# Graph layers on one core: attribute loads, table clears and window addresses moved ahead of the barrier behind the sorting

## The reference

```python
# layer 0, attention (edge_index = [src, dst], adj_vals = edge_weight)
h = x @ W
score = h[src] @ a_src + h[dst] @ a_dst
edge_e = exp(-leaky_relu(score, 0.2)) * adj_vals
h_prime = segment_sum(edge_e[:, None] * h[dst], src) / segment_sum(edge_e, src)
return elu(h_prime)
...
# layer 1, three rounds
for i in range(3):
    msg = relu(x[src] + edge_attr)
    aggr = segment_sum(msg, dst)
    h = relu(bn((x + aggr) @ W1[i] + b1[i]))
    x = bn(h @ W2[i] + b2[i])          # relu too, but for i = 2
```

## Time and profile before

| | us |
|---|---|
| median of 3 runs (lowest, highest) | 4825.21 (4821.34, 4827.64) |
| profiled execution, its own time | 4826.38 |
| its span | 4824.7 |
| PE busy, DVE busy, ACT busy, POOL busy | 4257.5, 4048.8, 2655.3, 3255.8 |
| sorting ends (ACT's last low, L841) | 793.7 |
| block 0 of the attention, first score | 810.1 |
| left-over step of the attention, DVE | 939.2 |
| end of the attention on PE | 2014.7 |

### The profile page before, as it was taken

How to read it: one execution, slowest core, us unless ns; L and a number is a source line. 1 busy time by engine, 2 the same in 40 slices (tenths; PEclk the granted TensorE clock), 3 DMA queues, 4 the chain that set the end, 5 groups by cost and what they waited for, 6 DMA issues and landing times.

```text
span 4824.7 us, 143705 instructions
## 1 busy us (share of the span) xinstructions
PE 4257.5 (88%) x50439; PEld 4143.0 (86%) x50440; DVE 4048.8 (84%) x7870; ACT 2655.3 (55%) x6749; POOL 3255.8 (67%) x2584
## 2 busy tenths in 40 slices
PE   2576676699999999789999997999999979999998
PEld 2566675699999999779999996999999969999996
DVE  7899996477777777678888887888888888888887
ACT  3899996377777777633344345334333454434434
POOL 0488883577777777557777773677777537777763
PEclk7777777799999999889999999999999989999999
DMA  9957663999899888678888884888888848888884
GB/s 123 263 187 242 205 217 124 306 251 251 248 249 250 252 249 248 176 239 278 281 280 279 280 280 149 265 280 281 278 277 281 265 151 279 281 279 280 280 281 148
DMA packets 664741, 1183.55 MB, mean 245 GB/s; under 512 B 151850, under 2 KB 489596, under 8 KB 664588
## 3 DMA queue, kind: packets, MB, share of 16 engines
q1 hardware_dynamic: 450204, 839.07, 53.1%
q10 hardware_dynamic: 133200, 176.14, 15.0%
q0 software_dynamic: 81184, 166.43, 11.0%
HBM read 967.32 MB, written 214.44 MB: 245 GB/s over the span
## 4 chain that ended last, share of the span: by engine, by line
PE 69%; DVE 16%; issue 6%; SPq 5%; DVEq 2%; ACT 1%; DMA 1%; POOL 0%; ACTq 0%; POOLq 0%; PEld 0%; PEldq 0%
PE ps L1766 23%; PE ps L1752 16%; PE ps L1681 12%; PE ps L1668 10%; PE ps L1776 6%; DVE sums L1159 2%; DVE field L1159 2%; DVE dst_hot L1452 2%; DVE sums L1460 2%; DVEq L1465 1%; SPq L552 1%; PE ps L1818 1%; DVE blk_hot L1151 1%; DVE scan L1196 1%; DVE rank L1213 1%
## 5 line engine op out<-in xcount | busy, mean ns | idle before, releaser
L774 POOL DMA_INDIRECT unit_x<-gin_rows,unit_src x1449 | 1785.1, 1232 | 701.8 <-PE ps L1766 456.8
L729 POOL DMA_INDIRECT attr_by_slot<-abuf,ridx x1080 | 1411.7, 1307 | 534.9 <-issue 327.4
L1766 PE MATMUL ps<-dst_hot,sums 128*128 128x128 f32 x10584 | 1519.8, 284 | 84.7 <-DVE agg L1467 84.7
L969 ACT ACTIVATE sums<-sums 128x512 f32<-128x512 f32 x1512 | 834.0, 572 | 1283.0 <-DVE sums L1460 1279.2
L1766 PEld LDWEIGHTS ps<-dst_hot,sums 128*128 128x128 f32 x10584 | 1306.4, 192 | 103.0 <-DVE agg L1467 86.1
L1752 PE MATMUL ps<-x_parts,src_turned 128*128 128x128 bf16 x15876 | 1143.0, 220 | 37.4 <-POOL x_parts L761 33.2
L1752 PEld LDWEIGHTS ps<-x_parts,src_turned 128*128 128x128 bf16 x15876 | 1026.8, 99 | 56.9 <-issue 41.6
L1460 DVE TENSOR_TENSOR sums<-ps,sums 128x512 f32<-128x512 f32 x1512 | 903.7, 615 | 131.2 <-PE ps L1752 127.5
L1452 DVE TENSOR_TENSOR dst_hot<-iota_one,dl_slot 128x896 f32<-128x896 f32 x756 | 818.2, 1082 | 2.2 <-DVE agg L1505 2.2
L881 ACT ACTIVATE val<-ps,val 128x128 f32<-128x128 f32 x2597 | 717.9, 375 | 185.2 <-DVE val L1305 185.2
L1681 PE MATMUL ps<-val,src_hot 128*128 128x129 f32 x5194 | 694.7, 283 | 2.2 <-DVE sums L1245 1.0
(11 more groups left out here) (243 smaller groups left out, 4361.3 us busy)
## 6 DMA issues: line engine op xcount, KB each, us to landing
sums<-attr_by_slot SPq DMA_DIRECT2D x756, 448.0 KB
src_turned<-rows_by_group SPq DMA_DIRECT2D x756, 224.0 KB
turned_hot<-rows_by_block ACTq DMA_DIRECT2D x392, 384.0 KB
attr_by_slot<-zeros SPq DMA_DIRECT2D x36, 3136.0 KB
unit_attr<-in_edge_attr SPq DMA_DIRECT2D x204, 448.0 KB
abuf<-in_edge_attr SPq DMA_DIRECT2D x72, 960.0 KB
unit_x<-gin_rows,unit_src POOLq DMA_INDIRECT x1449
attr_by_slot<-abuf,ridx POOLq DMA_INDIRECT x1080
```

Source lines behind the costliest of these rows:

```text
L729: pool.indirect_dma_start(out=attr_table, out_offset=bass.IndirectOffsetOnAxis(ap=ridx[:, g, t0 + t:t0 + t + 1], axis=0), in_=abuf[:, k % ...
L774: pool.indirect_dma_start(out=unit_x[:, half_place(k), t, :], out_offset=None, in_=gin_rows[n], in_offset=bass.IndirectOffsetOnAxis(ap=uni ...
L969: act.activation(attr[:, first:first + tiles, :], attr[:, first:first + tiles, :], ACT.Relu).then_inc(s_msg, 1)
L1766: ins = pe.matmul(ps[:, 7, 0:WINDOW], attr[:, b, :], dst_hot[:, HOT[c], b % G_TILES, :], start=(b == 0), stop=(b == BLOCKS - 1))
```

## The change

SORT_LOADS goes from 16 to 18, so loads 16 and 17 stand ahead of the barrier. LOADS_THEN goes from 19 to 20, so one more half is loaded and scattered ahead of the left-over step. The 34 clears are spread over the first 14 loads (CLEAR_LOADS) in place of 19. The first rows of the first 12 windows (HELD) behind the barrier are read into registers ahead of the waits.

```diff
-LOADS_THEN = 19
-SORT_LOADS = 16
+LOADS_THEN = 20
+SORT_LOADS = 18
+CLEAR_LOADS = 14
+HELD = 12
...
-            def load_windows(c):
+            def window_base(g):
+                return sp.value_load(base_i[0:1, g:g + 1], min_val=0, max_val=NODES - 1)
+
+            def load_windows(c, held={}):
                 for g in range(c * A_TILES, c * A_TILES + a_tiles(c)):
-                    base = sp.value_load(base_i[0:1, g:g + 1], min_val=0, max_val=NODES - 1)
+                    base = held[g] if g in held else window_base(g)
                     sp.dma_start(window_of(g), att_rows[bass.ds(window_at(base), WINDOW), :]).then_inc(s_win[c], 16)
...
                 if k == SORT_LOADS:
 
+                    held = {g: window_base(g) for g in range(EARLY * A_TILES, EARLY * A_TILES + HELD)}
                     sp.wait_ge(s_fld, GROUPS)
...
                     for c in range(EARLY, A_CHUNKS):
-                        load_windows(c)
+                        load_windows(c, held)
                 load_half(k)
-                for g in range(k * (BUCKETS - FILLS_FIRST) // LOADS_THEN, (k + 1) * (BUCKETS - FILLS_FIRST) // LOADS_THEN):
-                    clear_slots(g + FILLS_FIRST)
+                for g in range(k * (BUCKETS - FILLS_FIRST) // CLEAR_LOADS, (k + 1) * (BUCKETS - FILLS_FIRST) // CLEAR_LOADS):
+                    if g + FILLS_FIRST < BUCKETS:
+                        clear_slots(g + FILLS_FIRST)
```

## The result

| | before | changed |
|---|---|---|
| median of the runs (lowest, highest), us | 4825.72 (4821.34, 4827.64) | 4783.28 (4780.17, 4784.3) |
| ratio, 95% interval | | 0.9914 [0.9902, 0.9926] |
| profiled execution: its own time, span | 4826.38, 4824.7 | 4784.3, 4782.6 |

The change makes the kernel faster by 0.9%, 42 us; the forecast was 4778, 47 us. Lines behind the edit stand 7 further down (L1725 is now L1732, L1293 is L1300, L588 is L594).

The account below looks back on a forecast made before the run. PE was taken to stand 36.1 us before the left-over step for POOL's late gather, and block 0 to wait for windows; 36.1 + 8.0 + 3.0 = 47.1 us off 4825.2 gave 4778, own range 4773 to 4785.

Parts of the forecast that it names:

- Loads 16 and 17: SP's queue ahead of the barrier: issued at about 736 and 775 us, so POOL scatters on without waiting for data.
- The barrier: SP's wait ahead of the windows: still ends at 793 to 794 us; later than 795 would speak for starved scatters.
- Twelve reads ahead: SP's windows behind the barrier: end 8.5 us earlier, and block 0 of the attention gains 8.0, bounds 0 and 9.5.
- The rival of full engines: Block 0: DMA engines, not SP, set when windows land, so the reads bring nothing; gain 39.1 us, 4786, chance 9%.
- PE's wait: PE ahead of the left-over step: its whole wait of 36.1 us for POOL's gather goes.
- the clears: SP's queue in the sorting: denser clears hide under POOL's step with 5 us to spare, costed at nothing.
- The clock: PE behind the left-over step: without the hole, time at the lower clock goes too; 3.0 us, bounds 0 to 6.
- POOL's end: End of attention: POOL's scatters set it if POOL starts no earlier; gain 17 us, 4808, chance 3%.
- The late gather: Left-over step: four halves ahead of the gather make it late again; gain 40 to 47 us, up to 4785, chance 6%.
- the slower case: Sorting and barrier: denser clears starve POOL and delay load 17, barrier and windows; 4835 or more, chance 2%.
- no change: Whole kernel: the saved time comes back somewhere unseen, a change under 0.2%; chance 3%.

Follow-up runs that it names:

- g2: Changed kernel with POOL waiting until all slots are added before it scatters half 16, nothing left out: 4783.45 us, ratio 0.9914.
- g1: The kernel before, unchanged, run again for its profile: 4823.64 us (one run).
- g3: Kernel before with the clears over the first 14 loads and the 12 reads ahead, its loads unchanged: 4792.5 us, ratio 0.9934.
- g4: Changed kernel without POOL's scatters from half 20 on, 780 of 1080 left out: 4784.87 us, ratio 0.9918.
- e4: Kernel before with only the twelve reads ahead of the barrier, on the chip where the kernel before takes 5226 us: 5220.19 us, ratio 0.9987.
- e2: Kernel before with only the 34 clears spread over the first 14 loads, on the 5226 us chip: 5212.15 us, ratio 0.9967.

## Why the prediction was right, and where its sizes were off

The mechanism held, the sum was 6.4 us too large in the attention (47.1 against 40.7); the median, 4783.28, lies inside the forecast's own range of 4773 to 4785, 1.7 us from its upper end. The table splits the 40.7 into score 4.95, blocks 1 and 2 -0.24, idle 34.49 and rest 1.48.

**Loads 16 and 17** went early and met no barrier, as forecast; the last ended at 775.7 (775). POOL scattered from 774.4 to 816.5 without a hole (774 to 819).

**The barrier** opened at 795.1, against 793 to 794 forecast. That isn't starved scatters: the kernel before gives 794.56 in one execution and 795.49 in another, and holding the scatters back (g2) gives 794.23.

**Twelve reads ahead.** I took 8.5 us for SP and 8.0 for block 0. SP's windows went from 40.6 to 35.1 us: 5.5. Here one step failed, the guess that the old excess of the first 12 windows over their step was the reads' and would go as well: with the reads gone these 12 still take 804.5 - 795.1 = 9.4 us, and their DMA instruction itself takes 0.51 us at the median and up to 1.13 on SP, where that of the other windows takes 0.33. So even the 7.2 us of 12 x 0.6 didn't come whole. Block 0 gained 4.95 against the one profile of before and 6.41 against g1. From the first window's DMA to the last score it took 48.8 and 49.4 us before, and 42.6 to 43.7 in the four kernels with reads ahead, so 5 to 7 us is what the 12 reads give, at most 0.6 us each. The rival of full engines had foreseen no gain here; its share was 0.97 from 794 to 811 us and the windows landed in 3.2/4.0/6.6 us (min, median, max) where the earlier trace rows show 2.0/3.5/6.5, so the landing took back a part, not all. The rule of the Trainium skill that I weighed (DMA: Bandwidth & Descriptors, Issuing engines are not separate DMA queues) has that much in it here.

**PE's wait** was to go whole; 1.6 us stayed, in every kernel on the first chip that has the loads early. The trace puts it down to "issue". In the changed kernel DVE's first operation of the step is at 897.94 and its one-hot at 899.05, so DVE was ready for PE by then. The gather went at 881.6 (forecast 877), since data for half 18 were there at 839.35 in place of 835.4. It had 11 us to spare: in g3, where it is late, PE's product followed the second gather by 8.75 us, and 881.58 + 8.75 is 890.3.

**What removes the wait.** I gave the whole of it to the data that come earlier and costed the clears at nothing. That they cost nothing was right: SP issues a load and three clears in about 17 us in a step of 37.5, and POOL's idle time stays 0.30. That they bring nothing was wrong, and it was in my own rows: the full queues were read there. By g3 the clears and the reads alone take the gather to 899.0 and leave 11.4 us of the wait; only these are the loads'. In the medians that is 31.6 us and 9.1. (Between the two profiled executions it is 6.5: 9.75 less of the wait, and block 2 later by 3.57. Of that 1.98 is a later first window, and this start lies anywhere from 793.2 to 796.1 in the six executions, with early loads or without.) Clears and reads weren't run apart on this chip; by the table the reads' part is 5 to 7 us of the 31.6. Whether the loads alone would do as well as the clears alone wasn't tried there either.

**The clock** was to give 3.0 us, and gave nothing that can be told from the spread. Block 3 takes 918.07 - 903.35 = 14.7 us from chunk 0 to chunk 5 behind an idle time of 1.63, and 957.44 - 942.78 = 14.7 in g1, behind 32.77; the 15.9 of the profile that I used was 1.2 above what another execution of the same kernel shows, and g2, g3 and g4 show 15.0, 14.7 and 14.6. Timeline of DVE of g1:

```profile
942.78 0.18 DVE L1293 TENSOR_REDUCE z<-ps 128x6 f32<-128x24 f32 x1 [0.89 <-DVE sums L1375]
...
957.44 0.18 DVE L1293 TENSOR_REDUCE z<-ps 128x6 f32<-128x24 f32 x1 [0.52 <-PE ps L1670]
```

The step that failed is "without the hole this 3.0 goes too". The clock was lost without the long hole too: behind idle times of 1.63 and 3.10 us the granted clock is 0.50 from 905 to 909 and 1.00 again from 912 to 920 (0.77 from 905 to 920), and PE's group of 12 products takes 2.95 us at 908.4 and 1.59 at 912.6. The pause of 3.10 us stands behind the left-over step in the kernel before, in the changed one and in g3 alike, whether the step's data are late or not.

**POOL's end.** L736's last scatter was at 1943.6 (forecast 1938, before 2015.1), and 30 us ahead of the last sum. g4, without those scatters, took 4784.87: that rival is out. **The late gather** and **the slower case** didn't come; neither did no change, on this chip. On the other it did, by a way that isn't among my rivals: an engine whose own instructions come late, so that a wait for data is no longer what sets the step (in e4 the gather was issued 44 us before PE was done with block 2). The profile of before that I had shows no such gaps in the attention (PE busy for 400.00 of 400 us from 1200 to 1600), so nothing in it could tell.

## What to carry to other kernels

When one wait has two causes in series (data requested late, and a queue filled with work that nobody awaits yet), cost the removal of each alone before giving the gain to one: here the clears moved out of the way, with the reads, brought 31.6 us, and asking earlier the 9.1 that were left. Size small terms such as a clock's warm-up from two executions of the same kernel, not one: 1.2 us between them was two fifths of a term of 3. And a gain read from a wait holds only where that wait is there; the same kernel on a chip where PE stands for its own instructions gained nothing.

## What the runs showed that I had not expected

- The same kernel takes 4824 us on one chip and 5226 on another, at nearly the same mean granted clock (0.94 and 0.93). In the changed kernel PE's busy time between 1200 and 1600 us falls from 400.00 to 347.85 us, and idle pieces, in e2 of up to 2.4 us ahead of a single product, are put down to nothing that the profile shows. The page's rows of instruction queues are alike on both. The cause is open: that POOL's scatters bring it about is suggested by when the barrier opens, and wasn't shown, since the two kernels made for it (g2 and g4) ran where the gaps don't occur.
- The DMA of rows_by_group holds SP for 9.02 us behind queued clears (10.51 in e4); the same one takes 0.99 us in the changed kernel and in g3, with no clear ahead of it.
- POOL's indirect DMAs beside the attention cost PE nothing on the first chip: 780 of 1080 left out, and the time is 4784.87 against 4783.45 in g2.
